# Eight blocks of attention and an FP8 layer: POOL's order, two additions and the last layer's engines changed

## The chip, the cores and the metric

One core of one Trainium2 chip runs the whole program. Its engines work in parallel, each on its own list in order: PE (matrix multiplication, with weight loads listed as PEld), DVE (vector), ACT (scalar activations), POOL (GpSimd) and SP, which only issues transfers. Semaphores order them. The metric is the device time of one execution in microseconds (us).

## The reference, cut to what matters

```python
x = x + attention0(layernorm(x), ctx)
x = x + experts(layernorm(x))                      # top 2 of 8, gated MLP
# second attention, 16 heads of 16, 77 keys, on q = layernorm(x)
Qp = q @ Wq + bq;  Q = Qp / norm(Qp);  K = l2norm(ctx @ Wk + bk);  V = ctx @ Wv + bv
y = softmax(Q K^T * SCALE) V @ Wo + bo + Qp
x = x + (y - mean(y)) / sqrt(var(y) + eps) * gamma + beta
# last layer: FP8 matrix product, result rounded to bf16
xf = layernorm(x);  x8, sx = quant_fp8(xf);  w8, sw = quant_fp8(W)
x = x + ((x8 @ w8.T) * (sx * sw) + bias).astype(bfloat16)
```

x is 4 x 1024 tokens of 256 channels in f32, and stays on the chip as `g["x"]` (`x_res` in the trace).

## The kernel before, in words

The tokens are cut into `NBLK` = 8 blocks of 512 (`TJ` = 4 tiles of 128 tokens), two blocks to a batch (`BPB` = 2). The change touches two functions, `attention1` and `quantized_ffn`. Each writes, engine by engine, a fixed order of work for block n.

In `attention1` the blocks overlap. While PE works through the ten score and value steps (c = 0 to 9) of block n, it also projects the queries of block n+1 (`pe_queries`, L1805, c = 0 and 1), spreads the softmax sums of block n-1 (`pe_spread`, L1824, c = 2 to 4), transposes the queries of n+1 (`pe_transpose_q`, c = 4 and 5, L1783), makes the outputs of n-1 (`pe_outputs`, L1816, c = 5 and 6) and transposes the layer norm of n+2 (`pe_transpose_x`, c = 7 and 8, L1783). All transposes share one bank `tr`, so the second transpose waits until DVE's split (`dve_split`, L1949) has read the first (semaphore `tr_lo`).

DVE's order for block n (`dve_block`) is: shift of the last norm of n-3 (L2026), reciprocal of the sums (L1976), `dve_queries` (L1972) and `dve_combine` (L1957: adds the gathered experts' rows) in turns, the divides (L1984, L1988), statistics, `dve_shift` (L1966), the two query splits, maximum of the last norm (L2030), the residual of block n-1 (L1995), its statistics and gamma (L2009), one split of n+2, `dve_update` (L2017: x += y * rstd) and the other split. `dve_shift` waits for POOL's `gp_ln`.

POOL's order (`gp_block`) is: in the first block of a batch `gp_keys(.., 1)` (L2114, block-diagonal keys), `gp_beta` of n-1 (L2105), `gp_root` (L2095), in the second block of a batch `gp_keys(.., 0)`, four indirect gathers (L2084), `gp_ln` (L55, L57), four gathers, `gp_last_rstd`, `gp_residual` (L2101: qres = qp + bo) and `gp_y` (the 1/std of y). PE's order is not touched.

In `quantized_ffn`, for block n: ACT scales xf into v (`scaled`, L2290); DVE masks out the exponent (`power`, L2331); ACT makes of it the rounding constant (`round_at`, L2294); DVE adds and subtracts it (`rounded`, L2336 and L2339); PE transposes in f32 (L2380); ACT copies to bf16 (`copy_qT`, L2301); PE multiplies (L2391); DVE scales and adds the bias (`finish`, L2348); POOL adds to x (L2365); SP stores the block. v has three buffers, e, qT and z two each. ACT's order in one round is:

```python
round_at(n + 1)
scaled(n + 2)
copy_qT(n)
```

Of the kernel before, what the change touches and what calls it, by code (L numbers as in the profile page):

```python
# [1718 lines left out]
def attention1(nc, g, xd):  # L1719

    with ExitStack() as ctx:
# [198 lines left out]
        def act_block(act, n):  # L1920
            for c in range(NC3):
# [6 lines left out]
                if n > 2 and c in (0, 2):  # L1928
                    act_last_norm(act, n - 3, c // 2)
                if n < LAST and c in (1, 2):  # L1930
                    act_squares(act, n + 1, c - 1)
                if n < LAST and c == 3:
                    act_unit_queries(act, n + 1)
                if c == 4:
                    act_raw(act, n, 0)
# [32 lines left out]
        def dve_queries(dve, n, a):  # L1968
            dve.wait_ge(s["proj_mm"], proj_count(n, 0, a))
            if a == 0 and n >= 2:  # L1970
                dve.wait_ge(s["qres_ready"], n - 1)
            dve.tensor_tensor(pair(qp[n % 2], a), banked(proj), two_tiles(g["bq1"]), ALU.add).then_inc(s["proj_out"], 1)  # L1972

# [59 lines left out]
        def dve_block(dve, n):  # L2033
            nxt, nxt2, prv, prv2, prv3 = n < LAST, n + 1 < LAST, n > 0, n > 1, n > 2
            if prv3:
                dve_last_shift(dve, n - 3)
            if prv:
                dve_inverse_sums(dve, n - 1)
            if nxt:
                dve_queries(dve, n + 1, 0)  # L2040
            if nxt2:
                dve_combine(dve, n + 2, 0)
# [4 lines left out]
            if prv:  # L2047
                dve_divide(dve, n - 1, 0)
# [6 lines left out]
            if nxt2:  # L2055
                dve_shift(dve, n + 2)
            if prv:
                dve_divide(dve, n - 1, 2)
            if nxt:
                dve_split(dve, n + 1, 1, 0, qT[(n + 1) % 2])  # L2060
                dve_split(dve, n + 1, 1, 1, qT[(n + 1) % 2])
            if prv3:
                dve_last_max(dve, n - 3)
            if prv:
# [14 lines left out]
        def gp_gather(gp, n, ks=range(TOP_K)):  # L2079
            if n >= 2 and ks[0] == 0:  # L2080
                gp.wait_ge(s["both_added"], n - 1)
            for k in ks:
                for j in range(TJ):
                    gp.indirect_dma_start(out=routed[n % 2][:, k, j, :], out_offset=None, in_=xd,  # L2084
                                          in_offset=bass.IndirectOffsetOnAxis(ap=g["slots"][:, n, k, j:j + 1], axis=0)).then_inc(gathered[n % 2], 16)
# [12 lines left out]

        def gp_residual(gp, n):
            gp.wait_ge(s["proj_out"], max(proj_count(n, 0, 1), proj_count(n - 2, 1, 1) if n >= 2 else 0))  # L2100
            gp.tensor_tensor(qres[n % 2][:, :, :], qp[n % 2][:, :, :], four_tiles(g["bo1"]), ALU.add).then_inc(s["qres_ready"], 1)  # L2101

        def gp_beta(gp, n):
            gp.wait_ge(s["xn_ready"], n + 1)
            gp.tensor_tensor(g["x"][:, n, :, :], g["x"][:, n, :, :], four_tiles(g["beta"]), ALU.add).then_inc(s["beta_added"], 1)  # L2105
# [17 lines left out]
        def gp_block(gp, n):  # L2123
            nxt, nxt2, prv, prv2 = n < LAST, n + 1 < LAST, n > 0, n > 1
            if n % BPB == 0 and n:
                gp.wait_ge(s["score_mm"], NC3 * n)
                gp_keys(gp, n // BPB, 1)
            if prv:
                gp_beta(gp, n - 1)
# [5 lines left out]
            if n + 3 <= LAST:  # L2135
                gp_gather(gp, n + 3, range(0, 1))
            if nxt2:
                gp_ln(gp, n + 2)
            if n + 3 <= LAST:
                gp_gather(gp, n + 3, range(1, TOP_K))  # L2140
            if prv2:
                gp_last_rstd(gp, n - 2)
            if prv:
                gp_residual(gp, n)
                gp_y(gp, n - 1)

        with nc.Block() as block:  # L2147
            @block.gpsimd
            def _(gp):
# [8 lines left out]
                gp_residual(gp, 0)  # L2158
                for n in range(NBLK):
                    gp_block(gp, n)  # L2160
                gp_beta(gp, LAST)
# [28 lines left out]
            def _(dve):  # L2190
# [6 lines left out]
                for a in range(2):  # L2197
                    dve_queries(dve, 0, a)
                for k in range(TOP_K):
# [16 lines left out]
                for a in range(2):  # L2216
                    dve_residual(dve, LAST, a)
                    dve_y_stats(dve, LAST, a)
                    dve_gamma(dve, LAST, a)
                dve_update(dve, LAST)  # L2220
# [24 lines left out]

def quantized_ffn(nc, g, w, out):

    with ExitStack() as ctx:
        sb = lambda name, shape, dt: ctx.enter_context(nc.sbuf_tensor(name, shape, dt))
        pb = lambda name: ctx.enter_context(nc.psum_tensor(name, [P, 512], F32))  # L2250
        bias = sb("ffn_bias", [P, D], F32)
# [5 lines left out]
        qT = [sb(f"ffn_qT{s}", [P, DC, TB], BF16) for s in range(2)]  # L2257
        z = [sb(f"ffn_z{s}", [P, TJ, D], BF16) for s in range(2)]
        tr = [pb(f"ffn_tr{s}") for s in range(2)]
# [3 lines left out]
                 "tr_mm", "qT_out", "mm", "z_out", "x_done", "stored")  # L2263
        s = {n: ctx.enter_context(nc.semaphore(n + "4")) for n in names}

# [6 lines left out]
        with nc.Block() as block:  # L2272
            @block.sync
            def _(sp):
                sp.dma_start(bias[:, :], w["L1_ffn_bias"].partition_broadcast(P)).then_inc(s["bias_in"], 16)
# [6 lines left out]

            @block.scalar
            def _(act):
                def scaled(n):
                    if n >= 3:
                        act.wait_ge(s["tr_mm"], DC * (n - 2))
# [6 lines left out]
                def copy_qT(n):  # L2296
                    if n >= 2:
                        act.wait_ge(s["mm"], 2 * n - 2)
                    for dc in range(DC):
                        act.wait_ge(s["tr_mm"], DC * n + dc + 1)  # L2300
                        act.activation(qT[n % 2][:, dc, :], tr[dc][:, :], ACT.Copy).then_inc(s["qT_out"], 1)  # L2301

                act.wait_ge(s["limit_done"], 8)
                scaled(0)
                round_at(0)
                scaled(1)
                for n in range(NBLK):
# [4 lines left out]
                    copy_qT(n)  # L2312

            @block.vector
            def _(dve):
# [9 lines left out]
                dve.wait_ge(s["bias_in"], 16)  # L2325
# [8 lines left out]
                def rounded(n):  # L2334
                    dve.wait_ge(s["m_ready"], n + 1)
                    dve.scalar_tensor_tensor(values(v[n % 3]), values(e[n % 2]), ROUND_AT * FP8_MIN_NORMAL, values(v[n % 3]),  # L2336
                                             ALU.add, ALU.add).then_inc(s["t_done"], 1)
                    dve.wait_ge(s["t_done"], n + 1)
                    dve.scalar_tensor_tensor(values(v[n % 3]), values(e[n % 2]), ROUND_AT * FP8_MIN_NORMAL, values(v[n % 3]),  # L2339
                                             ALU.add, ALU.subtract).then_inc(s["q_ready"], 1)  # L2340

                def finish(n):
                    if n >= 2:
                        dve.wait_ge(s["x_done"], n - 1)
                    for a in range(2):
                        dve.wait_ge(s["mm"], 2 * n + a + 1)
                        for b in range(2):
                            last = dve.scalar_tensor_tensor(z[n % 2][:, 2 * a + b, :], acc[2 * (n % 2) + a][:, b * D:(b + 1) * D],  # L2348
                                                            dequant[:, 0:1], bias[:, :], ALU.mult, ALU.add)
                        last.then_inc(s["z_out"], 1)  # L2350

                power(0)
                for n in range(NBLK + 1):
                    if n + 1 < NBLK:
                        power(n + 1)
                    if n < NBLK:
                        rounded(n)
                    if n >= 1:
                        finish(n - 1)

            @block.gpsimd
            def _(gp):
                for n in range(NBLK):
                    gp.wait_ge(s["z_out"], 2 * n + 2)
                    gp.tensor_tensor(g["x"][:, n, :, :], g["x"][:, n, :, :], z[n % 2][:, :, :], ALU.add).then_inc(s["x_done"], 1)  # L2365

            @block.tensor
            def _(pe):
# [3 lines left out]
                ffn_spread_scales(pe, g, small, scale_row, s["small_mm"])  # L2372

                def transposes(n):
                    pe.wait_ge(s["q_ready"], n + 1)
                    for dc in range(DC):
                        if n >= 1:
                            pe.wait_ge(s["qT_out"], DC * (n - 1) + dc + 1)
# [74 lines left out]
```

## Time and profile before

| what | us |
|---|---|
| median of 3 runs | 1111.58 (1111.31 to 1115.03) |
| the profiled execution | 1118.64 |
| span of its instructions | 1116.8 |
| second attention, first to last block's PE work | about 757 to 1016 of the span |
| its tail, until the last layer begins | to 1053.8 |
| last layer, until its last addition ends | 1053.8 to 1113.8 |
| store of the last block | to 1116.8 |

Times in the rows count from the start of the span. Mean duration overlaps for neighbouring instructions; the step from start to start is what a series costs.

### The profile page before, as it was taken

How to read it: one execution, taken by the hardware profiler on the slowest of the kernel's cores; microseconds unless marked ns; L12 is line 12 of the kernel's file. 1: busy time of each engine (PE TensorE's matmuls, PEld its weight loads, DVE VectorE, ACT ScalarE, POOL GpSimd, SP SyncE). 2: the span in 40 equal slices, each digit the busy share in tenths (PEclk: the TensorE clock that was granted, in tenths of full speed). 3: DMA queues.
4: the chain of work that ended last, by engine and by line, in shares of the span. 5: the costliest groups of instructions: out<-in, count | busy, mean ns of one | idle time of the engine just before them, and what ended most of it. 6: DMA issues, size and time to landing. Idle time of an engine off the chain costs nothing. (4 is left out here: it accounts for less than half of the span.)

```text
span 1116.8 us, 17792 instructions
## 1 busy us (share of the span) xinstructions
PE 937.9 (84%) x5479; PEld 776.5 (70%) x5479; DVE 795.3 (71%) x1838; ACT 536.7 (48%) x1471; POOL 393.6 (35%) x418
## 2 busy tenths in 40 slices
PE   5999999999997999989999975337979889996254
PEld 5899999999996888878999965224445545543143
DVE  6788788788875678766777765333488688777497
ACT  4676566665664554424444431025545465642252
POOL 3243234243343365450000012464455665222024
PEclk9899999999999899999999996558899899997555
DMA  9999910000000343223344332120001110000012
GB/s 304 286 304 301 301 49 0 0 0 0 0 1 29 95 132 114 92 75 105 119 121 127 119 112 44 54 58 24 28 25 38 38 38 1 0 1 1 5 56 95
DMA packets 52758, 91.97 MB, mean 82 GB/s; under 512 B 5350, under 2 KB 27726, under 8 KB 52686
## 3 DMA queue, kind: packets, MB, share of 16 engines
q1 hardware_dynamic: 46542, 74.29, 22.2%
q0 software_dynamic: 6144, 16.79, 4.7%
q8 instruction: 38, 0.62, 0.2%
q14 instruction: 34, 0.28, 0.1%
HBM read 34.69 MB, written 56.36 MB: 82 GB/s over the span
## 5 line engine op out<-in xcount | busy, mean ns | idle before, releaser
L462 POOL TENSOR_TENSOR prob<-prob,row_inv 128x462 f32<-128x462 f32 (+1 forms) x96 | 83.6, 874 | 184.9 <-DVE row_inv L623 184.9
L794 PE MATMUL acc<-u,probT 128*128 128x256 f32 (+1 forms) x960 | 133.5, 289 | 0.9 <-DVE u L635 0.9
L522 ACT ACTIVATE prob<-score,neg_max 128x77 f32<-128x77 f32 x512 | 120.6, 348 | 13.2 <-DVE neg_max L617 12.9
L748 PE MATMUL score<-m,xnT 128*128 128x462 f32 (+1 forms) x576 | 124.8, 355 | 0.0
L794 PEld LDWEIGHTS acc<-u,probT 128*128 128x128 f32 (+1 forms) x960 | 119.4, 189 | 1.9 <-DVE u L635 1.4
L748 PEld LDWEIGHTS score<-m,xnT 128*128 128x128 f32 x576 | 97.7, 191 | 6.3
L1057 PE MATMUL py<-w1T,hidT 128*128 x426 | 92.6, 353 | 0.0
L1324 POOL DMA_INDIRECT dispatched<-xn,slots x64 | 68.7, 1073 | 61.0 <-DVEq L1189 43.9
L512 ACT ACTIVATE probT<-tr 128x512 fp32r<-128x512 f32 (+1 forms) x96 | 51.5, 541 | 68.7 <-PE tr L734 68.5
L1835 PE MATMUL score<-qT,kbd 128*128 128x512 f32 (+1 forms) x240 | 80.2, 444 | 2.1 <-ACT prob L1903 2.1
L2084 POOL DMA_INDIRECT routed<-dispatched,slots x64 | 62.4, 975 | 40.8 <-SPq L2147 22.9
L1057 PEld LDWEIGHTS py<-w1T,hidT 128*128 128x128 f32 x426 | 71.8, 191 | 0.2 <-issue 0.2
L617 DVE TENSOR_REDUCE neg_max<-score 128x6 f32<-128x462 f32 (+1 forms) x96 | 55.8, 581 | 17.4 <-PE score L748 16.9
L1846 PE MATMUL acc<-prob,va 128*102 128x512 f32 x128 | 66.9, 606 | 0.0
L612 DVE TENSOR_TENSOR probT<-tr,probT 128x512 fp32r<-128x512 f32 (+1 forms) x96 | 56.5, 592 | 14.0 <-ACT probT L512 13.6
L1835 PEld LDWEIGHTS score<-qT,kbd 128*128 128x128 f32 (+1 forms) x240 | 41.7, 193 | 30.0 <-ACT prob L1903 15.5
L1611 POOL MEMSET head_rows<- 128x616 f32 x1 | 0.6, 611 | 166.9 <-POOLq L1327 166.9
L621 DVE TENSOR_REDUCE row_sum<-prob 128x6 f32<-128x462 f32 (+1 forms) x96 | 55.3, 576 | 3.0 <-ACT prob L522 2.1
L1903 ACT ACTIVATE prob<-score 128x512 f32<-128x512 f32 (+1 forms) x80 | 45.8, 584 | 16.8 <-PE score L1835 16.8
L734 PE MATMUL tr<-ident,prob 128*128 128x128 f32 x320 | 50.0, 272 | 1.0 <-DVE probT L612 1.0
L1135 ACT ACTIVATE gated<-py 128x192 f32<-128x192 f32 x71 | 23.5, 331 | 41.1 <-PE py L1057 41.1
L734 PEld LDWEIGHTS tr<-ident,prob 128*128 128x128 f32 x320 | 38.9, 138 | 6.0 <-issue 1.2
(323 smaller groups left out, 2273.9 us busy)
## 6 DMA issues: line engine op xcount, KB each, us to landing
dispatched<-zeros SPq DMA_DIRECT2D x1, 33664.0 KB, 118.6
xn<-dispatched SPq DMA_DIRECT2D x71, 128.0 KB, 2.1
dispatched<-hid SPq DMA_DIRECT2D x71, 128.0 KB, 1.7
out<-x_res SPq DMA_DIRECT2D x8, 512.0 KB, 2.6
x_res<-in_x SPq DMA_DIRECT2D x1, 3072.0 KB, 15.2
w_stage<-in_L_ffn_W SPq DMA_DIRECT2D x8, 384.0 KB
w_stage<-in_L_ffn_Ws SPq DMA_DIRECT2D x3, 384.0 KB
x_res<-in_x SPq DMA_DIRECT2D x2, 512.0 KB, 10.1
```

Source lines behind the costliest of these rows:

```text
L462: gp.tensor_tensor(pr, pr, row_inv[t % 2][:, heads(k)].unsqueeze(2).to_broadcast([P, BANK_HEADS[k], KEYS]), ALU.mult).then_inc(prob_ready, 1)
L522: last = act.activation(prob[t % 2][:, h * KEYS:(h + 1) * KEYS], score_of(t, k)[:, n * KEYS:(n + 1) * KEYS], ACT.Exp, bias=neg_max[t % 2][ ...
L612: dve.tensor_tensor(probT[t % 2][1][:, c0:c0 + n, :], tr_of("p", t, gr)[:, 0:n * P].rearrange("p (c q) -> p c q", q=P), f32(probT[t % 2][0 ...
L617: dve.tensor_reduce(neg_max[t % 2][:, heads(k)], scores_of(t, k), AX_X, ALU.max, negate=True).then_inc(max_ready, 1)
L734: last = pe.transpose(tr_of("p", t, gr)[0:w, (c - c0) * P:(c - c0 + 1) * P], prob[t % 2][:, c * P:c * P + w], g["ident"][:, :])
L748: last = pe.matmul(score_of(t, k)[:, 0:BANK_HEADS[k] * KEYS], xnT[blk][i][:, dc, j * P:(j + 1) * P], m[w][:, dc, cols(k)], start=(n == 0 a ...
L794: last = pe.matmul(acc[t % 2][:, 0:D], probT[t % 2][i][0:rows, c, :], u[k][0:rows, c, :], start=(c == 0 and q == 0), stop=(c == KCH - 1 an ...
L1057: last = pe.matmul(py[i % 2][:, 0:UP], xtT[i % 2][m][:, dc, :], w1[k][:, dc, ds(expert, 1), :].rearrange("p a h -> p (a h)"), start=(q == ...
L1324: gp.indirect_dma_start(out=xd, out_offset=bass.IndirectOffsetOnAxis(ap=g["slots"][:, n, k, j:j + 1], axis=0), in_=xn[n % XN_BUFS][:, j, : ...
L1835: last = pe.matmul(score[c % 2][0:rows, :], keys, qT[n % 2][k][:, f, :], start=(q == 0), stop=(q == 2))
L1846: last = pe.matmul(acc[f][0:A_COLS, :], g["va"][0:rows, b, f, cc, :], p, start=(cc == 0), stop=(cc == A_LAST))
L2084: gp.indirect_dma_start(out=routed[n % 2][:, k, j, :], out_offset=None, in_=xd, in_offset=bass.IndirectOffsetOnAxis(ap=g["slots"][:, n, k, ...
```

## The change

1. `attention1`, additions: `gp_beta` and `gp_residual` go. DVE makes both in one instruction each: `dve_query_residual(n)` before the first divide, `dve_beta(n-1)` after the second gamma. For block 0 the residual stands ahead of DVE's combine of block 1.
2. `attention1`, POOL's order: the second keys wait also for `x_done` (the update before). In the second block of a batch no gather stands ahead of `gp_ln`; in others two, not four. `gp_y` comes ahead of the last gathers of a second block and ahead of `gp_last_rstd`.
3. `attention1`, DVE and ACT order: `dve_last_shift` after the first queries, `dve_shift` between the two query splits (it was ahead of both); on ACT the last norm goes from c = 0, 2 to c = 1, 3, behind squares and unit queries.
4. `quantized_ffn`: rounding writes bf16 (`q`), transposes are bf16 into a bf16 bank of 1024 columns, all eight ahead of one semaphore; ACT copies them in one instruction and also applies the scale and writes z. The bias enters through PE as a third matmul per tile, from three bf16 pieces that POOL makes of it once. DVE adds z to x. PE's order is `transposes(n)` and then `products(n-1)`.

```diff
 def dve_block(dve, n):
-    if prv3: dve_last_shift(dve, n - 3)
     if prv: dve_inverse_sums(dve, n - 1)
     if nxt: dve_queries(dve, n + 1, 0)
+    if prv3: dve_last_shift(dve, n - 3)
...
     if prv:
+        dve_query_residual(dve, n)
         dve_divide(dve, n - 1, 0)
...
-    if nxt2: dve_shift(dve, n + 2)
     if prv: dve_divide(dve, n - 1, 2)
     if nxt: dve_split(dve, n + 1, 1, 0, qT[(n + 1) % 2])
+    if nxt2: dve_shift(dve, n + 2)
     if nxt: dve_split(dve, n + 1, 1, 1, qT[(n + 1) % 2])
...
         dve_gamma(dve, n - 1, 1)
+        dve_beta(dve, n - 1)
 def gp_block(gp, n):
     if n % BPB == 0 and n:
+        gp.wait_ge(s["x_done"], n - 1)
         gp.wait_ge(s["score_mm"], NC3 * n)
         gp_keys(gp, n // BPB, 1)
-    if prv: gp_beta(gp, n - 1)
     if nxt: gp_root(gp, n + 1)
-    if nxt and n % BPB == BPB - 1:
+    if turn:                               # nxt and n % BPB == BPB - 1
         gp.wait_ge(s["score_mm"], NC3 * n + C3)
         gp_keys(gp, n // BPB + 1, 0)
-    if n + 3 <= LAST: gp_gather(gp, n + 3, range(0, 1))
+    elif nxt3: gp_gather(gp, n + 3, 0, 2)
     if nxt2: gp_ln(gp, n + 2)
-    if n + 3 <= LAST: gp_gather(gp, n + 3, range(1, TOP_K))
+    if nxt3: gp_gather(gp, n + 3, 0 if turn else 2, 6 if turn else TOP_K * TJ)
+    if prv: gp_y(gp, n - 1)
+    if nxt3 and turn: gp_gather(gp, n + 3, 6)
     if prv2: gp_last_rstd(gp, n - 2)
-    if prv:
-        gp_residual(gp, n)
-        gp_y(gp, n - 1)
 # quantized_ffn, POOL (was: x += z for every block)
+    gp.memset(bias_rows[:, :], 0.0); gp.memset(minus_one[:, :], -1.0)
+    gp.wait_ge(s["limit_done"], 7)
+    gp.tensor_scalar(part, bias, scales[0:1, 0:1], g["ffn_w_scales"][0:1, 0:1], ALU.mult, ALU.mult)
+    for n, at in enumerate(BIAS_AT):       # (0, 32, 64); each step waits for the one before
+        gp.tensor_copy(piece[n], part)
+        gp.tensor_copy(bias_rows[at:at + 1, :], piece[n])
+        if n + 1 < len(BIAS_AT): gp.tensor_tensor(part, part, piece[n], ALU.subtract)
 # ACT, one round
     round_at(n + 1); scaled(n + 2); copy_qT(n)
+    if n: finish(n - 1)    # 2 x activation(z, acc, ACT.Copy, scale=dequant), 128x512
 # DVE, one round
-    power(n + 1); rounded(n); finish(n - 1)
+    rounded(n); power(n + 2); add(n - 2)   # add: x = x + z, 128x1024
 # PE, products(n), for each of four tiles
     for dc in range(DC): matmul(bank, qT[n % 2][:, j, dc, :], g["ffn_wqT"][:, dc, :], ...)
+    if n == 0 and j == 0: pe.wait_ge(s["part_step"], PART_STEPS)   # 9
+    matmul(bank, minus_one[:, :], bias_rows[:, :], start=False, stop=True)
 # PE, one round
-    products(n - 1); transposes(n)
+    transposes(n); products(n - 1)
```

## Rows read from the trace of the kernel before

**Rows 1.** Windows, six blocks of the second attention, a tail stretch, the last layer.

```profile
core 0: us, PE busy (x) PEld busy (x) DVE busy (x) ACT busy (x) POOL busy (x), PEclk, DMA share, GB/s
764.98:793.99 29.01, 25.15 (x95) 14.70 (x95) 9.84 (x24) 15.26 (x36) 12.73 (x13) 0.88 0.12 36
793.99:829.33 35.34, 29.98 (x118) 16.97 (x117) 26.03 (x47) 17.03 (x38) 22.11 (x20) 1.00 0.10 31
829.33:861.27 31.94, 29.91 (x116) 16.81 (x117) 27.07 (x56) 15.70 (x36) 17.55 (x18) 1.00 0.12 33
861.27:899.85 38.58, 32.64 (x117) 18.97 (x117) 28.89 (x57) 18.34 (x41) 23.32 (x22) 0.91 0.10 28
899.85:931.89 32.04, 30.16 (x117) 16.72 (x117) 27.65 (x57) 18.21 (x41) 17.56 (x18) 1.00 0.11 34
931.89:964.41 32.52, 30.02 (x116) 16.81 (x117) 28.77 (x57) 18.21 (x41) 15.37 (x14) 1.00 0.00 1
1030.00:1040.00 10.00, 7.58 (x17) 5.00 (x16) 5.24 (x11) 2.07 (x4) 0.00 (x0) 0.50 0.00 0
1053.80:1113.80 60.00, 31.34 (x131) 21.34 (x131) 49.85 (x66) 26.47 (x32) 19.79 (x8) 0.50 0.16 64
```

**Rows 2.** Waits of PE, 764 to 1012: total us, times, longest.

```profile
PE tr L1783 <- DVE qT L1949: 11.3, 5, 3.5
PE proj L1805 <- DVE xnT L1949: 5.8, 5, 1.6
PE proj L1805 <- DVE qp L1972: 2.8, 5, 0.6
```

**Rows 3.** Timeline of DVE: start us, us, then the idle time before and its releaser.

```profile
811.19 0.16 DVE L1966 SCALAR_TENSOR_TENSOR shift<-mean_var,rstd 128x4 f32<-128x4 f32 x1 [5.28 <-POOL rstd L57]
...
856.75 3.77 DVE L2017 SCALAR_TENSOR_TENSOR x_res<-y,rstd_y,x_res 128x256 f32<-128x256 f32 x4
...
893.05 6.05 DVE L2017 SCALAR_TENSOR_TENSOR x_res<-y,rstd_y,x_res 128x256 f32<-128x256 f32 x4
...
1043.30 1.67 DVE L2017 SCALAR_TENSOR_TENSOR x_res<-y,rstd_y,x_res 128x256 f32<-128x256 f32 x4 [0.50 <-POOL rstd_y L57]
```

**Rows 4.** Timeline of POOL beside those updates.

```profile
856.69 2.37 POOL L2105 TENSOR_TENSOR x_res<-x_res,beta 128x1024 f32<-128x1024 f32 x1
...
892.98 2.93 POOL L2114 TENSOR_TENSOR kbd<-k1T,head_rows 128x616 fp32r<-128x616 f32 x2
```

**Rows 5.** Groups by form: busy us, mean ns of one.

```profile
L1663 DVE TENSOR_TENSOR k<-k,kinv 77x1024 f32<-77x1024 f32 x1 | 1.2, 1222 | 0.0
...
L1400 POOL CAST first_row<-first_i 1x71 f32<-1x71 int32 x1 | 0.2, 233 | 0.0
```

**Rows 6.** Timeline of ACT and PE, start and tail of the second attention.

```profile
754.06 2.08 ACT L1894 ACTIVATE xn<-x_res,shift,rstd 128x256 f32<-128x256 f32 x4 [3.66 <-DVE shift L1966]
...
1022.38 2.01 PE L1824 MATMUL wide<-oinv,spread_sum 6*96 6x512 f32 x2 [6.32 <-DVE oinv L1976]
```

**Rows 7.** Timeline of the last layer, all engines.

```profile
1061.42 1.22 DVE L2336 SCALAR_TENSOR_TENSOR ffn_v<-ffn_e,ffn_v 128x1024 f32<-128x1024 f32 x1
1061.53 1.15 ACT L2294 ACTIVATE ffn_e<-ffn_e,floor 128x1024 f32<-128x1024 f32 x1 [0.76 <-DVE ffn_e L2331]
1063.95 1.97 PE L2380 MATMUL ffn_tr<-ident,ffn_v 128*128 128x128 f32 x8 [7.76 <-DVE ffn_v L2339]
1065.95 0.60 ACT L2301 ACTIVATE ffn_qT<-ffn_tr 128x512 bf16<-128x512 f32 x1 [0.26 <-PE ffn_tr L2380]
1066.61 1.89 PE L2391 MATMUL ffn_acc<-ffn_wqT,ffn_qT 128*128 128x256 bf16 x8 [0.69 <-ACT ffn_qT L2301]
...
1069.33 0.68 DVE L2331 TENSOR_SCALAR ffn_e<-ffn_v 128x1024 int32<-128x1024 int32 x1
1069.49 2.50 POOL L2365 TENSOR_TENSOR x_res<-x_res,ffn_z 128x1024 f32<-128x1024 f32 x1 [21.27 <-DVE ffn_z L2348]
1069.93 3.15 DVE L2336 SCALAR_TENSOR_TENSOR ffn_v<-ffn_e,ffn_v 128x1024 f32<-128x1024 f32 x1
...
1111.67 2.12 POOL L2365 TENSOR_TENSOR x_res<-x_res,ffn_z 128x1024 f32<-128x1024 f32 x1 [1.82 <-DVE ffn_z L2348]
```

**Rows 8.** Timeline of PE: where the clock rose, and where it did not.

```profile
757.39 1.12 PE L1783 MATMUL tr<-ident,qn 128*128 128x128 f32 x4 [5.82 <-DVE qT L1949]
758.16 2.81 PE L1835 MATMUL score<-qT,kbd 128*128 128x512 f32 x6
...
1031.62 3.75 PE L1816 MATMUL proj<-wo1f,oT 128*128 128x256 f32 x8 [1.57 <-DVE oT L1988]
1036.23 3.78 PE L1816 MATMUL proj<-wo1f,oT 128*128 128x256 f32 x8 [0.85 <-DVE y L1995]
```

More of the change, by code:

```diff
@@ L1933, in act_block @@
                     act_unit_queries(act, n + 1)
+                if n > 2 and c in (1, 3):
+                    act_last_norm(act, n - 3, c // 2)
                 if c == 4:
@@ L2076, in dve_block, with gp_gather @@
                 dve_split(dve, n + 2, 0, 1, xnT)
-        def gp_gather(gp, n, ks=range(TOP_K)):
-            if n >= 2 and ks[0] == 0:
+        def gp_gather(gp, n, first=0, last=TOP_K * TJ):
+            if n >= 2 and first == 0:
                 gp.wait_ge(s["both_added"], n - 1)
[L2082 to L2085, printed above, removed]
+            for k, j in (divmod(i, TJ) for i in range(first, last)):
+                gp.indirect_dma_start(out=routed[n % 2][:, k, j, :], out_offset=None, in_=xd,
+                                      in_offset=bass.IndirectOffsetOnAxis(ap=g["slots"][:, n, k, j:j + 1], axis=0)).then_inc(gathered[n % 2], 16)
         def gp_ln(gp, n):
@@ L2250, in quantized_ffn @@
         pb = lambda name: ctx.enter_context(nc.psum_tensor(name, [P, 512], F32))
-        bias = sb("ffn_bias", [P, D], F32)
+        bias, part = sb("ffn_bias", [1, D], F32), sb("ffn_bias_part", [1, D], F32)
+        piece = [sb(f"ffn_bias_piece{i}", [1, D], BF16) for i in range(len(BIAS_AT))]
+        bias_rows, minus_one = sb("ffn_bias_rows", [BIAS_END, D], BF16), sb("ffn_minus_one", [BIAS_END, P], BF16)
+        ident = sb("ffn_ident", [P, P], BF16)
         amax, limit, scale_row = ffn_scale_buffers(sb, "x")
@@ L2311, in _ @@
                         scaled(n + 2)
-                    copy_qT(n)
+                    if n < NBLK:
+                        copy_qT(n)
+                    if n:
+                        finish(n - 1)
             @block.vector
@@ L2340, in rounded, with add @@
+                    dve.scalar_tensor_tensor(values(q[n % 2]), values(e[n % 2]), ROUND_AT * FP8_MIN_NORMAL, values(v[n % 3]),
                                              ALU.add, ALU.subtract).then_inc(s["q_ready"], 1)
[L2342 to L2350, printed above, removed]
+                def add(n):
+                    dve.wait_ge(s["z_out"], 2 * n + 2)
+                    dve.tensor_tensor(x_values(g["x"], n), x_values(g["x"], n), values(z[n % 2]), ALU.add).then_inc(s["x_done"], 1)
@@ L2352, in _ @@
                 power(0)
-                for n in range(NBLK + 1):
-                    if n + 1 < NBLK:
-                        power(n + 1)
+                power(1)
+                for n in range(NBLK + 2):
                     if n < NBLK:
                         rounded(n)
[L2358 to L2365, printed above, removed]
+                    if n + 2 < NBLK:
+                        power(n + 2)
+                    if n >= 2:
+                        add(n - 2)
```

128 lines of the change are left out of this document (80 added, 48 removed).

## The prediction, made before the changed kernel was run

> **What bounds the kernel now.** I cut the span into stages with the windows view and read which wait ends last in the two stages that the change touches. In the second attention [rows 1] PE is busy 25.15 to 32.64 us of blocks that last 29 to 38.6 us, so PE sets the pace and what can be won is its idle time. Over the six blocks: 3.9, 5.4, 2.0, 5.9, 1.9 and 2.5 us. The clock column adds to this: it is 0.88 in the first and 0.91 in the fourth block. The fourth does the same work as its neighbours but is busy 32.64 us against about 30.0, so 2.6 us are work at 1.2 in place of 2.4 GHz, right behind one of the long gaps; the first lost about as much (0.12 of 29 us at half speed, some 3). PE's waits name three causes [rows 2]: the query transpose waits for DVE's split (11.3 us in 5 waits), the projection waits for the split of the layer norm (5.8) and for the reading of its bank (2.8).
>
> The timeline of DVE says why DVE is late. `dve_shift` sits ahead of the query splits and waits up to 5.28 us for POOL's rstd [rows 3], behind keys and four gathers. And `dve_update` takes 1.67 us at the end, where POOL is idle, but 3.77 beside POOL's 2.37 us addition of beta, and 6.05 beside keys and beta together [rows 3, 4]: POOL's large two-input instructions hold DVE up nearly for their whole length (2.1 of 2.37 us; 4.4 of about 5.3, the two of them one behind the other). The Trainium skill (GPSIMD Engine Reference, 1. Specifications) says that POOL shares its SBUF interfaces with DVE instructions that read two SBUF inputs; by that rule the trace agrees, 3.77 against 1.67 us.
>
> In the last layer (60 us) DVE is busy 49.85, PE 31.34 at half clock, ACT 26.47 [rows 1]. DVE sets its pace, and it too is held up: the first rounding step takes 1.22 us alone and 3.15 beside POOL's 2.50 us addition [rows 7].
>
> **The change, part by part: second attention.**
> *Shift moved.* The first query split no longer stands behind POOL. Of the first, second and fourth block it frees 2.6, 3.4 and 3.4 us of PE (most of the 11.3 [rows 2]; the rest, twice 0.8, is a divide that the shift had delayed). With the gaps the two stretches at the low clock go: 2.2 and 2.6 us (of the 3 in the first block I count 2.2).
> *Additions moved to DVE.* The trace has no such DVE instruction; the nearest is a two-input f32 multiply of 77x1024, 1.22 us [rows 5], 1.15 from start to start. Per block DVE gets 2.3 us and loses 2.1 (update without beta), and 4.4 in the three blocks where keys stood there too, as the keys now wait for the update. So the split behind the update comes 2.1 - 1.15 = 0.95 us earlier in a common block, 4.4 - 1.15 = 3.2 in those three. The waits of the projection there were 0.4 to 0.6 and 1.6 us long [rows 2], and the 0.6 us wait for the bank follows from the same lateness: all 8.6 us can go. The residual lies where DVE waited for PE's spread anyway. If POOL's keys meet it, it grows; lower bound 1.15, upper 1.15 + 2.1.
> *New bound.* I took DVE's list of the fifth block (32.0 us from reciprocal to reciprocal, about 27.6 busy [rows 1]) and put the change in: 32.0 + 2.3 - 2.1 - 1.2 (a gamma that had run beside the residual) - 0.8 (shift wait) = 30.2 us, against PE's 30.2. A tie, so I leave each block 0.4 to 0.8 us above PE's sum. Gains by block: 4.8, 5.1, 1.4, 7.6, 1.5, 1.9, and 0.7 for the seventh, sum 23.0. Two engines that are both full make waits that I don't see; I take 15% off: 19.5.
> *Start.* Ahead of block 0, the residual stands in front of combine(1), statistics, shift and ACT's norm, for which ACT waited 3.66 us before it could copy the queries [rows 6]: all path, +1.15.
> *Tail.* PE waits 6.32 us for the reciprocal behind the update of block 6 [rows 6]. Beta costs 1.15 there, hides the 0.5 that the update waited for POOL, and the update falls by 2.1: -1.45. In block 7 beta is new on the path, less the same 0.50 [rows 3]: +0.65. Net -0.8.
> *Gathers.* 2 of 8 now come behind `gp_y` in a second block; they start about 2 us ahead of the next block and are needed 4 us into it, so 6 us cover two issues of 1.26 and their landing. Costed at nothing; uncovered, they would add up to 2 us in two blocks. The keys are needed by step c = 5, some 15 us off: nothing. ACT's moved norm: nothing, its consumer stands last.
> Second attention: -19.5 + 1.15 - 0.8 = -19.2.
>
> **Last layer.** Prices, start to start [rows 7]: scaled S and round_at R 1.05 (seen 1.15 later), DVE power 0.6 (0.68), rounding pair 2.5 (2 x 1.22), add 1.15 (as above), copy C of 1024 columns 1.05 (S's size; two of 0.60 were 1.2), finish F twice 0.6. Products: 8 matmuls took 1.89 us, so 12 take 2.75. Transposes: unseen in bf16. Upper bound the f32 row, 1.97; lower bound half a 256-column bf16 matmul each (1.89/16 x 8 = 0.95). I take 1.1, near the lower, as the bf16 matmul row fits the type.
> I laid these on the four lists by hand. DVE's own sum is 4.3 us a block and ACT's 4.15, but a loop through all engines is longer: S(n) ends, power 0.7, add 1.1, rounded(n-1) 2.55, transposes 1.1, products(n-2) 2.7, its F 0.5, R 1.05, S(n+2) 1.15 = 10.85 us for two blocks, 5.4 each, where now it is 60/8 = 7.5 with start and end, 6.5 in between. The stamps, in the old span's time: first rounding done 1062.25 (it was 1063.9), S(6) done 1082.85, rounded(6) 1091.55, rounded(7) 1095.25, transposes(7) 1096.5, products 1101.9, last F 1102.5, last addition 1103.7. Before it was 1111.67 + 2.12 = 1113.8 [rows 7]: -10.1.
> *Bias pieces.* Nine steps of POOL, 256 elements each: between 0.23 us (a 1x71 cast [rows 5]) and 0.6 (a quarter of 2.37 [rows 4]) plus 0.1. They end 3.0 to 6.3 us behind 1056.4, ahead of the first products at 1066.6, so PE doesn't wait. But they run beside the first rounding (from 1059.75) and may hold it up by 0 to 2.5 us. I take 1.5, as the rounding has two SBUF inputs like the update: -8.6 in all.
>
> **Sum.** -19.2 - 8.6 = -27.8. On the profiled execution 1118.64 - 27.8 = 1090.8; that one lies 7.1 us above the median of the runs, and I take the same difference off the median: 1111.58 - 27.8 = 1083.8.
>
> **The rivals.**
> *R1, PE's clock rises in the last layer.* New rounds give PE two runs of 3.8 us with a 0.6 us gap, then 2.7 idle. For it: ahead of the first block PE worked from 757.39 to 760.97 without a gap, and the first block then starts at the high clock. Against it: two runs of 3.75 and 3.78 us with a gap of 0.85 stayed at 0.50 [rows 8, 1], the nearer picture. With the clock up, transposes save 0.5 and products 1.35 per two blocks of the loop, 4 x 1.85 = 7.4, and some 1.5 in the tail: about 1075. The Trainium skill (TensorE: Matmul & The Clock Gate, What's actually happening) says that activity releases the throttle; by that rule both rows can be read, since the second is broken up.
> *R2, only part of the waits goes.* DVE with 29 us in 30.2 becomes the bound and gives half of the 23 back, or the last layer's transposes cost 1.97 (+0.9 x 4 + 0.9 = 4.5): 1089 to 1100. For it the tie of 30.2 and 30.2; against it the three big gaps, which don't depend on DVE's load.
> *R3, the other side: the additions on DVE are stretched themselves.* They read two SBUF inputs, and POOL still makes keys. If they were held up in every block to 3.3 us each (1.2 + 2.1), DVE would gain 6.6 and lose 2.1: +4.5 in seven blocks, +31, against -10 (shift), -5 (clock), -8.6: 1119. It decides from 3.4 us net per block ((10 + 5 + 8.6)/7). Against it: POOL's large instructions after the change are only the keys, 2.7 us in six places, so most blocks have nothing that could do it. By the skill's rule above, the sum would be 3 x 2.1 = 6 us worse at most.
> *R4, nothing that can be measured*: a new wait per block of 3 to 4 us in POOL's list (for `x_done`, or `gp_y` ahead of gathers) that eats the gain.
>
> **How the numbers follow.** The forecast (1077 to 1091 its own range) 0.56; R1 0.15; R2 0.19; R3 and other losses 0.05; R4 0.05. The range leaves out 1 in 10 above and the far end of R1 below: 1073 to 1098. A difference under 0.5% (5.6 us) can't be told from none. Faster than 1106: 0.90; within 0.5%: 0.05; slower: 0.05.
>
> **What would show it.** In the second attention: PE's waits for the query split near 0 (were 11.3), clock 1.00 in all blocks, blocks of 30 to 31 us, the update at 1.67 throughout. In the last layer: rounds of 5.4 us, both rounding steps at 1.22 but for the first block, PEclk 0.50. Wrong: the update still over 3 us; additions over 2 us; DVE's share over 0.95 with PE waiting on it; rounds of 6 us or more, or a last layer at clock 1.00.

## The result, and the profile after

The changed kernel takes 1072.2 us (median of 4 runs, 1068.67 to 1077.18) against 1113.3 for the kernel before beside it: ratio 0.9634, 95% interval 0.9589 to 0.968. Timed again in another set it was 1080.3 against 1116.2, ratio 0.9658 (0.9633 to 0.9682). So it gains 36 to 41 us where 27.8 were forecast; the first median lies 0.8 us under the range.

The profiled execution took 1071.32 us. The second attention, from its first gather to the maximum that opens the last layer (`x_amax`), took 344.1 us before and 319.1 after; the last layer, from there to its last addition, 60.0 and 46.8. That makes -38.1 us. The code ahead of the first gather is the same in all kernels; that gather started at 709.7 us before, at 700.4 here, and at 703.6 to 711.3 in the twelve other profiles. So the 9.3 us between the two profiles there can't be put down to the change.

Windows of the changed kernel, its first six blocks by the first projection of each, and the last layer (compare [rows 1]):

```profile
756.94:781.32 24.38, 22.23 (x95) 13.39 (x95) 9.83 (x24) 15.25 (x36) 10.34 (x12) 1.00 0.15 44
781.32:811.09 29.77, 29.55 (x119) 16.87 (x117) 23.71 (x49) 15.99 (x37) 16.81 (x18) 1.00 0.12 36
811.09:840.99 29.90, 29.70 (x119) 16.90 (x117) 25.53 (x57) 16.17 (x38) 14.71 (x17) 1.00 0.13 36
840.99:871.01 30.02, 29.81 (x119) 16.81 (x117) 26.65 (x59) 18.14 (x42) 16.81 (x19) 1.00 0.12 36
871.01:901.00 29.99, 29.78 (x118) 16.79 (x117) 26.60 (x59) 18.08 (x42) 15.97 (x18) 1.00 0.12 36
901.00:931.02 30.02, 29.77 (x119) 16.83 (x117) 26.64 (x59) 18.10 (x41) 10.31 (x12) 1.00 0.00 1
1019.56:1066.41 46.85, 21.53 (x163) 15.82 (x163) 36.47 (x42) 34.87 (x41) 8.41 (x11) 0.75 0.18 70
```

Read the second and third number of each line together. From the second block on PE is busy for all but 0.2 us of a block, at full clock; in the first it is still idle for 2.15 us, 1.6 of them in one gap. Against [rows 1] the blocks gained 4.6, 5.6, 2.0, 8.6, 2.1 and 2.5 us, 25.4 in all.

PE's waits in the second attention (compare [rows 2], which begins later, at the first block). The 7.1 us of the first line, 2.8 of the second, the 1.4 and the 0.8 stand ahead of that block; behind it 0.3 us are left of the first line and 0.5 of the second:

```profile
PE tr L1783 <- DVE qT L1949: 7.4, 2, 7.1
PE tr L1783 <- DVE xnT L1949: 3.3, 5, 1.4
PE proj L1805 <- DVE xnT L1949: 1.4, 1, 1.4
PE proj L1805 <- DVE qp L1972: 0.8, 1, 0.8
```

DVE's timeline, the end of one block: beta, the two splits and the update between them (compare [rows 3]), and POOL's line that answers to [rows 4], the keys that now wait for the update:

```profile
925.81 1.21 DVE L1980 TENSOR_TENSOR x_res<-x_res,beta 128x1024 f32<-128x1024 f32 x1
926.94 0.68 DVE L1949 TENSOR_TENSOR xnT<-tr,xnT 128x512 fp32r<-128x512 f32 x1
927.54 1.66 DVE L2025 SCALAR_TENSOR_TENSOR x_res<-y,rstd_y,x_res 128x256 f32<-128x256 f32 x4
929.25 0.69 DVE L1949 TENSOR_TENSOR xnT<-tr,xnT 128x512 fp32r<-128x512 f32 x1
```

```profile
929.28 2.73 POOL L2116 TENSOR_TENSOR kbd<-k1T,head_rows 128x616 fp32r<-128x616 f32 x2 [1.12 <-DVE x_res L2025]
```

The update takes 1.66 or 1.67 us in every block, the new additions 1.21 to 1.23.

The start and the tail, ACT and PE (compare [rows 6, 8]):

```profile
746.08 2.07 ACT L1894 ACTIVATE xn<-x_res,shift,rstd 128x256 f32<-128x256 f32 x4 [4.97 <-DVE shift L1966]
```

```profile
987.36 2.02 PE L1824 MATMUL wide<-oinv,spread_sum 6*96 6x512 f32 x2 [4.98 <-DVE oinv L1984]
...
996.60 3.75 PE L1816 MATMUL proj<-wo1f,oT 128*128 128x256 f32 x8 [1.57 <-DVE oT L1996]
1001.21 3.78 PE L1816 MATMUL proj<-wo1f,oT 128*128 128x256 f32 x8 [0.85 <-DVE y L2003]
```

From first gather to first projection of block 1 it is 56.5 us, against 55.3; from 931.0 to `x_amax` 88.5, against 89.4.

The last layer, two rounds of ACT and the transposes beside them (compare [rows 7]):

```profile
1037.20 1.14 ACT L2316 ACTIVATE ffn_v<-xf,scales 128x1024 f32<-128x1024 f32 x1
1038.24 1.01 ACT L2326 ACTIVATE ffn_qT<-ffn_tr 128x1024 bf16<-128x1024 bf16 x1
...
1042.64 0.98 PE L2408 MATMUL ffn_tr<-ffn_ident,ffn_q 128*128 128x128 bf16 x8 [4.96 <-DVE ffn_q L2377]
...
1045.00 0.69 ACT L2333 ACTIVATE ffn_z<-ffn_acc,dequant 128x512 bf16<-128x512 f32 x1 [0.32 <-PE ffn_acc L2424]
...
1046.97 0.62 PE L2408 MATMUL ffn_tr<-ffn_ident,ffn_q 128*128 128x128 bf16 x8 [0.79 <-DVE ffn_q L2377]
...
1047.84 1.14 ACT L2316 ACTIVATE ffn_v<-xf,scales 128x1024 f32<-128x1024 f32 x1
```

From the first `ffn_v` to the last shown two blocks take 10.64 us. They are a slow round and a quick one: DVE's second rounding step starts 6.33 us behind the one before it, then 4.33. In the slow round PE does its transposes at the low clock (0.98 us at 1042.64, behind a wait of 4.96), in the quick one at the high clock (0.62 at 1046.97). The three stretches of the last layer, up to the first rounds, the body, and behind the last rounding step:

```profile
1022.56:1034.56 12.00, 3.63 (x25) 2.87 (x26) 10.08 (x10) 9.41 (x10) 7.78 (x9) 0.50 0.00 0
1034.56:1060.56 26.00, 13.89 (x105) 9.93 (x103) 20.71 (x20) 21.44 (x26) 0.00 (x0) 0.84 0.24 97
1060.56:1066.56 6.00, 3.27 (x32) 2.65 (x32) 4.06 (x4) 3.34 (x5) 0.00 (x0) 1.00 0.35 141
```

The clock did not stay at 0.50: it moves between its two levels (1.2 and 2.4 GHz) in the body and is at the high one in the tail.

### The profile page after: what moved, and what is told of

Same layout as the page of the kernel before. It is cut to its first block and busy times, and to the rows that moved or that the text cites. A ratio compares the mean times of both kernels' runs of the same rounds, so it can differ in the third digit from the quotient of the medians.

```text
span 1069.6 us, 17855 instructions
## 1 busy us (share of the span) xinstructions
PE 916.8 (86%) x5511; PEld 764.3 (71%) x5511; DVE 775.9 (73%) x1830; ACT 544.2 (51%) x1480; POOL 350.9 (33%) x405
## 5 line engine op out<-in xcount | busy, mean ns | idle before, releaser
L522 ACT ACTIVATE prob<-score,neg_max 128x77 f32<-128x77 f32 x512 | 121.0, 351 | 11.6 <-DVE neg_max L617 11.3
L1324 POOL DMA_INDIRECT dispatched<-xn,slots x64 | 70.2, 1097 | 55.9 <-DVEq L1189 38.8
L612 DVE TENSOR_TENSOR probT<-tr,probT 128x512 fp32r<-128x512 f32 (+1 forms) x96 | 56.5, 592 | 14.0 <-ACT probT L512 13.6
L621 DVE TENSOR_REDUCE row_sum<-prob 128x6 f32<-128x462 f32 (+1 forms) x96 | 55.3, 576 | 3.1 <-ACT prob L522 2.2
```

The costliest lines, as they stand in the source:

```text
L522: last = act.activation(prob[t % 2][:, h * KEYS:(h + 1) * KEYS], score_of(t, k)[:, n * KEYS:(n + 1) * KEYS], ACT.Exp, bias=neg_max[t % 2][ ...
L612: dve.tensor_tensor(probT[t % 2][1][:, c0:c0 + n, :], tr_of("p", t, gr)[:, 0:n * P].rearrange("p (c q) -> p c q", q=P), f32(probT[t % 2][0 ...
L1324: gp.indirect_dma_start(out=xd, out_offset=bass.IndirectOffsetOnAxis(ap=g["slots"][:, n, k, j:j + 1], axis=0), in_=xn[n % XN_BUFS][:, j, : ...
```

## The experiments

Stage times below are as above, from one profile each: second attention, last layer (344.1 and 60.0 in the kernel before; 319.1 and 46.8 in the changed kernel, 318.8 and 46.9 when it was profiled again).

**The two halves alone.**

```diff
 # first run: attention1 as changed, quantized_ffn as before
 # second run: attention1 as before, quantized_ffn as changed
```

> The second attention as changed, the last layer as before. Theory A (the gains of the two stages are separate and add): the second attention, from its first gather to the start of the last layer, takes 319 us as in the changed kernel (344 before), the last layer 60 us as before; in all 25 us less than before, a ratio near 0.978. Theory B (the forecast's tie: the two full engines leave only 19 us to win, and the rest of the measured gain came from elsewhere): stage of 325 us, ratio 0.983. Theory C (the 9 us that the untouched stages differ by in the two profiles belong to the change): they differ here again by about 9 us.

> The last layer as changed, the second attention as before. Theory A (the stages add): last layer 47 us, second attention 344 us, in all 13 us less than before, ratio 0.988. Forecast's size: 51.4 us, ratio 0.992. Theory C (untouched stages belong to the change): they are 9 us shorter here too.

Measured: 1090.74 us (ratio 0.9803, 0.9775 to 0.983), stages 318.9 and 60.0; and 1098.76 (0.9872, 0.9842 to 0.9901), stages 340.9 and 47.1. Beside them the kernel before had 1114.12. The halves don't touch each other: -23.4 and -15.4 make -38.8. Each is more than its part of the forecast, 19.2 and 8.6. The 340.9 us are the attention of the kernel before, unchanged, and 3.2 less than in its other profile: PE's clock was 0.88 in the first block there and 1.00 here, and the second output projection of the tail took 3.78 us there and 1.99 here. Against this profile the attention gained 22.0 us and not 25.0. The second run's last layer also shows what the clock is worth in it:

```profile
1060.58:1086.58 26.00, 17.49 (x103) 12.32 (x102) 20.56 (x20) 20.97 (x25) 0.00 (x0) 0.57 0.23 94
1086.58:1092.58 6.00, 3.99 (x36) 2.83 (x34) 4.29 (x4) 4.24 (x7) 0.00 (x0) 0.93 0.34 139
```

The body ran at 0.57 in place of 0.84 and the layer took 47.1 us in place of 46.8. What differs is the quick rounds: their transposes took 1.03 us here and 0.62 there, where PE had time to spare. The slow rounds had theirs at the low clock in both.

**The shift's old place.**

```diff
+    if nxt2: dve_shift(dve, n + 2)        # ahead of the last divide and both splits again
     if prv: dve_divide(dve, n - 1, 2)
-    if nxt2: dve_shift(dve, n + 2)        # it stood between the splits
 # POOL: gp_ln behind four gathers in every block again
```

> The changed kernel with two parts of the order undone: the shift stands ahead of the last divide and both query splits again, and four gathers stand ahead of POOL's layer norm. Theory A (the split waited for POOL's rstd): PE's wait for the query split comes back, about 11 us in five waits (the changed kernel has 0.3 us there after block 0's start), with one or two stretches at the low clock, and the second attention takes 330 to 333 us in place of 319. Rival B (the moved additions alone had made DVE late, and with them settled the shift has slack): under 3 us more.

Measured: 1089.57 us, second attention 333.5, 14.4 more. One block of it, and PE's waits:

```profile
852.59:887.70 35.11, 31.03 (x119) 17.99 (x117) 26.86 (x59) 18.23 (x42) 16.90 (x19) 0.95 0.10 31
```

```profile
PE tr L1783 <- DVE qT L1949: 20.1, 6, 7.1
```

The waits for the query split go from 7.4 to 20.1 us, and with each of the two longest (3.9 us) PE does the same work in 31.0 to 31.2 us in place of 29.8 or less, at clock 0.95. These two parts of the order, the shift's place and POOL's gathers, were undone together, so their shares are not known; together they are worth over half of the 25 us.

**Both additions on POOL, in the new order.**

```diff
-    dve_query_residual(dve, n); dve_beta(dve, n - 1)
 # gp_block, behind the second keys, and ahead of gp_y
+    if prv: dve_beta(gp, n - 1)
+    if prv: dve_query_residual(gp, n)
```

> The changed kernel with beta and the residual made by POOL again, the rest of the order as changed. Theory A (POOL's large two-input instructions hold DVE's updates up): the update takes 3.8 us beside beta and 1.7 nowhere but at the end, PE waits for the split of the layer norm and for its bank come back, 5 to 9 us in all, second attention 324 to 328 us. Rival B (with the keys moved away from the update, DVE has the slack to bear 2.1 us): the updates are long but PE waits under 2 us, second attention 319 to 321 us. Rival C (the additions cost DVE more than they give back): under 319 us.

Measured: 1077.75 us, second attention 315.7, 3.5 less than with DVE's additions. My theory, that the update would be held up again, was wrong. DVE's update, two of its gammas, POOL's beta and residual, and the block that grew most:

```profile
838.40 2.37 DVE L2017 SCALAR_TENSOR_TENSOR y<-y,mean_var_y,gamma 128x256 f32<-128x256 f32 x2
...
843.96 1.67 DVE L2025 SCALAR_TENSOR_TENSOR x_res<-y,rstd_y,x_res 128x256 f32<-128x256 f32 x4
...
898.58 3.51 DVE L2017 SCALAR_TENSOR_TENSOR y<-y,mean_var_y,gamma 128x256 f32<-128x256 f32 x2
```

```profile
845.29 2.58 POOL L1980 TENSOR_TENSOR x_res<-x_res,beta 128x1024 f32<-128x1024 f32 x1
...
899.04 2.36 POOL L1976 TENSOR_TENSOR qres<-qp,bo 128x1024 f32<-128x1024 f32 x1
```

```profile
877.56:908.60 31.04, 29.48 (x119) 16.87 (x117) 28.22 (x57) 17.99 (x40) 22.76 (x21) 1.00 0.12 35
```

Before, `gp_y` was POOL's last work in a block; it released the update and POOL went straight to beta. In the new order `gp_last_rstd` stands between, and in the blocks with second keys those wait for the update and beta stands behind them. Beta starts 1.33 us behind the update, near its end, and doesn't hold it up. The collisions moved elsewhere: four of the gammas beside POOL's residual took 1.65 to 3.51 us, where 0.9 is usual, and two shifts of the last norm 1.94 and 2.32 in place of 0.15. With DVE's additions all of these took 0.88 to 0.92 and 0.10 to 0.16. All in all the six blocks grew by 1.0 us; the 3.5 us less lie ahead of them and in the tail, and the last comparison below says why.

**The keys don't wait for the update.**

```diff
     if n % BPB == 0 and n:
-        gp.wait_ge(s["x_done"], n - 1)
```

> The changed kernel without the wait for the update ahead of POOL's second keys, so that the keys come back beside the update in three blocks. Theory A (large two-input POOL work beside the update is what stretched it): the update of those three blocks takes 3.5 to 4.5 us in place of 1.67. If the split behind it sets PE's start, the second attention grows by 3 to 6 us (319 to 322 to 325); if DVE has 2 us of slack there, it stays at 319 to 320 though the update is long.

Measured: 1082.46 us, second attention 324.9. Two of the three updates concerned are held up; the first, and POOL's keys beside it:

```profile
814.88 4.76 DVE L2025 SCALAR_TENSOR_TENSOR x_res<-y,rstd_y,x_res 128x256 f32<-128x256 f32 x4
...
937.14 3.94 DVE L2025 SCALAR_TENSOR_TENSOR x_res<-y,rstd_y,x_res 128x256 f32<-128x256 f32 x4
```

```profile
816.61 2.73 POOL L2116 TENSOR_TENSOR kbd<-k1T,head_rows 128x616 fp32r<-128x616 f32 x2
```

Those blocks last 31.7 and 31.2 us in place of 29.8 and 30.0. The stretch ahead of block 1 takes 29.4 in place of 27.5, at clock 0.50, but it took 29.3 and 29.4 in two profiles with the attention as changed as well; so the wait for `x_done` is worth 3.8 us of the 5.8 (from block 1 to block 7, 177.9 us in place of 174.1). The middle update kept its 1.66 us: two gathers and `gp_last_rstd` stood ahead of the keys there, which began 3.06 us behind it. In the other two only the gathers or only `gp_last_rstd` stood between, and the keys began 1.73 and 0.59 us behind the update. So a delay alone is no sure remedy: beta, in the experiment above, began 1.33 us behind the update and left it alone, and the keys at 1.73 did not.

The update ends 0.3 us behind the end of the keys. The Trainium skill (SBUF — State Buffer, Who interferes with whom) says that a DVE instruction with two SBUF inputs and a POOL instruction that reads SBUF exclude each other, and that the order of issue decides which of the two waits. On the first point these rows agree. The order can't be read from them: of the update's four instructions the last was held up (3.57 us), and the profile has it start at 816.06, 0.55 us ahead of the keys.

**Four more additions on DVE.**

```diff
     dve_beta(dve, n - 1)
+    for i in range(4): dve.tensor_tensor(spare, two_tiles(gamma), two_tiles(bo1), ALU.add)   # 128x512
```

> The changed kernel with four more two-input additions of 128x512 on DVE, each waiting for the one before, behind beta in every block from the second on: about 2.8 us of DVE work a block that nobody needs. The forecast's step (DVE and PE are tied at 30.2 us, so every us on DVE is a us of the block): blocks of 32.5 to 33 us in place of 30.0, second attention 335 to 340 us. Theory A (DVE's waits for PE shrink as it gets later, DVE is busy 26.6 of 30 us and PE alone sets the block): blocks of 30.0 to 31 us, second attention 320 to 326 us.

Measured: 1108.36 us, second attention 345.8, 26.6 more, above both of my ranges. One block (from 822.0), and PE's waits over four blocks:

```profile
822.00:856.00 34.00, 31.07 (x116) 17.72 (x116) 28.06 (x61) 16.27 (x36) 16.80 (x18) 0.95 0.12 35
```

```profile
PE tr L1785 <- DVE xnT L1951: 11.7, 4, 2.9
```

The four add 2.8 us of DVE's time and the block grows by 4.1: the split behind them is late by 2.9, where PE had waited for it 0.3 us in four blocks together, and the other 1.2 are PE's lower clock behind the gap. DVE is busy 26.6 of 30 us in the changed kernel and has all the same nothing to spare at this place. The tie that the prediction worked out (30.2 against 30.2) was real at this place; it cost nothing by itself.

**In the last layer, ScalarE's order and PE's clock.**

```diff
 # first run: six idle products a round, into a bank of their own
     products(n - 1)
+    for _ in range(6): matmul(warm, ffn_wqT[:, 0, 0:128], ffn_wqT (512 columns))
 # second run: finish one block later
-    copy_qT(n); finish(n - 1)
+    finish(n - 2); copy_qT(n)
```

> The changed kernel with six bf16 matmuls of 512 columns into a spare bank behind each block's products in the last layer, to fill PE's idle time; they change no result. If PE's clock, which goes up and down there (1.2 GHz in the transposes and products behind each long gap), costs time on the loop through all engines: the clock stays high from the third block on and the last layer takes 42 to 44 us in place of 46.9. If the high clock is not kept, or the filling delays the transposes: 48 to 52 us.

> The changed kernel with ACT finishing block n-2 ahead of the copy of block n, where it finished n-1 behind it; so ACT no longer waits for products that PE has just begun. If the loop through all engines (10.6 us for two blocks) sets the pace of the last layer, and not the clock or DVE's own sum: rounds of 4.4 to 4.6 us (DVE's sum 4.3), last layer 40 to 43 us in place of 46.9. If DVE or ACT alone was the bound already: 46 to 47.5 us.

Measured: 1075.86 us with a last layer of 44.3 us, and 1081.07 with 43.7, each a little above the range I had for its theory. The body of each in two windows of 10 us, from 15 us behind `x_amax` on (first run, then second):

```profile
1041.62:1051.62 10.00, 7.23 (x57) 4.52 (x55) 8.12 (x8) 9.18 (x13) 0.00 (x0) 1.00 0.16 66
1051.62:1061.62 10.00, 6.67 (x53) 4.23 (x52) 9.12 (x10) 9.28 (x11) 0.00 (x0) 1.00 0.34 137
```

```profile
1047.43:1057.43 10.00, 6.90 (x45) 4.79 (x43) 8.78 (x9) 9.36 (x12) 0.00 (x0) 0.67 0.22 88
1057.43:1067.43 10.00, 7.42 (x45) 5.22 (x45) 9.35 (x10) 9.23 (x12) 0.00 (x0) 0.55 0.31 123
```

With the clock up all through the body, the layer gains 2.5 us. All of it lies in two slow rounds, 7.03 and 6.33 us before, 5.96 and 4.89 now; the quick ones stay at 4.33, DVE's own sum. What the idle products cost by standing ahead of the next transposes was not measured apart. With the finish behind the next block's work the rounds are 4.33 and 4.71 us at a clock of 0.55 to 0.67, with DVE busy 0.9 of the time: ScalarE's waits for PE's products, 2.4 us in the body of the changed kernel, are gone, and with them, as the last comparison shows, nearly all that the clock could give.

**POOL adds z to x in the last layer.**

```diff
-    add(n - 2)                            # DVE
+    for n in range(NBLK): ...             # waits for both halves of z(n), then
+                          gp.tensor_tensor(x[n], x[n], z[n % 2], ALU.add)   # POOL, behind the bias pieces
```

> The changed kernel, but in the last layer POOL adds z to x again, as before the change, in place of DVE. Theory: the addition on POOL (2.1 to 2.5 us) holds up DVE's rounding steps (3.15 in place of 1.22 us), so that DVE gains 1.2 us a block and loses about 2: last layer 50 to 54 us in place of 46.9, with rounding steps above 2.5 us in most blocks. Rival: the loop through ScalarE and PE sets the round (DVE is busy 7.1 to 7.7 of 10 us), so the stretching is hidden and the last layer stays at 46 to 49 us.

Measured: 1085.16 us, last layer 50.05, at the low end of my range, and not for its reason. Only one rounding step met an addition:

```profile
1065.75 3.15 DVE L2380 SCALAR_TENSOR_TENSOR ffn_q<-ffn_e,ffn_v 128x1024 bf16<-128x1024 f32 x1
```

```profile
1065.70 2.12 POOL L2312 TENSOR_TENSOR x_res<-x_res,ffn_z 128x1024 f32<-128x1024 f32 x1 [1.67 <-ACT ffn_z L2336]
...
1076.13 4.20 POOL L2312 TENSOR_TENSOR x_res<-x_res,ffn_z 128x1024 f32<-128x1024 f32 x2 [0.66 <-ACT ffn_z L2336]
```

The last rounding step ended 41.0 us into the layer, 0.5 earlier than with DVE's additions; the loss is the end, 9.0 us behind it in place of 5.3. Of these 3.7 us the two slower additions are 1.8 (4.20 against 2.38); the rest goes with PE's clock, 0.82 there and 1.00 in the changed kernel. In the runs with the shift's old place and with four more additions the last layer was unchanged, and its end took 6.1 us at clock 0.86: 0.8 us for the clock alone.

**A version from the parts that won, and the changed kernel beside it.** The first is the changed kernel as it is, the second has both additions on POOL and the later finish, the third the idle products besides.

> The changed kernel once more, untouched, as the measure for the two versions beside it. If the 41 us that it won over the kernel before (1113.3 to 1072.2) are its stages' 38.1 us (344.1 to 319.2 and 60.0 to 46.9) and 3 us of chance in the parts ahead of the second attention, this run gives 1074 to 1077 against 1114. If the change itself made those early parts shorter, it gives 1070 to 1072, and the second attention begins at 700 us again; by chance it begins anywhere from 700 to 711.

> The changed kernel with two edits at once: POOL makes both additions again (as in the run that put the second attention at 315.6 us, 3.6 less than the change), and ScalarE finishes block n-2 ahead of the copy of block n (which put the last layer at 43.8 us, 3.1 less). If both hold, the time is 6 to 7 us under the changed kernel timed beside it, a ratio near 0.994 to it, attention stage 315 to 317 and last layer 43.8. If the 3.6 us were the chance of one look (its clock rose once early, ahead of the first block, worth about 1.3), attention stays at 318 to 319 and the gain is 3 to 4 us.

> The same two edits and six idle matrix products (512 columns each, into a bank of their own) behind the products of every round of the last layer. Alone they took 2.5 us off the last layer (46.9 to 44.4), the later finish 3.1. If both work on the same loop (the products' time ahead of ScalarE's finish), they don't add: the last layer stays at 43 to 44 us, near DVE's own sum of 4.3 us a block, or gets longer because the idle products stand ahead of the next transposes. If they are separate: 41.3 us.

| kernel | us, median | ratio to before (1116.2) | second attention | last layer |
|---|---|---|---|---|
| as changed | 1080.32 (5 runs) | 0.9658 (0.9633 to 0.9682) | 318.8 | 46.9 |
| additions on POOL, later finish | 1076.51 (5 runs) | 0.9638 (0.9616 to 0.9659) | 317.3 | 43.7 |
| the same, idle products | 1074.85 (6 runs) | 0.9612 (0.9589 to 0.9636) | 319.8 | 43.2 |

The untouched changed kernel came out above the 1074 to 1077 us that I had expected; its stages are those of the first profile, and its second attention began at 710.1 us. The last layer keeps its 3 us; the idle products add 0.5 more, not 2.5, as DVE now goes round in 4.33 us, its own sum. The 3.5 us of the attention don't hold: with the additions on POOL the stage came out at 315.7, 317.3 and 319.8. The difference between these is where the clock rises. In the last of them the two output projections at the tail took 3.75 and 3.78 us, as in the changed kernel; in the other two the second took 1.99. And in the first of them the stretch ahead of block 1 took 24.9 us at clock 0.73, in the other two 26.5 and 26.6. The third version has no such luck; against the changed kernel profiled beside it, it saves 0.7 us up to block 1 (PE waits 5.82 for the query split, not 7.13) and loses 1.1 in the blocks and 0.5 in the tail. The intervals of the first and the third version overlap by 0.0003; the second's overlaps with both.

## Why the prediction was right or wrong

The direction, the places and most of the mechanisms were right; the gain was forecast 10 us too small, against 38 in the traces. By its steps:

- *Shift moved*: right. 11.3 us of waits became 0.3, the stretches at the low clock went, and putting it back, with POOL's gathers, cost 14.4 us, against 9.4 + 4.8 forecast.
- *Additions moved to DVE*: price right (1.21, and 1.13 from start to start), the update right (1.66 everywhere), cause wrong. I put the 2.1 us a block that the update lost down to the beta on POOL, and so to its move. With beta on POOL and POOL's new order the update is 1.67 too. The gain belongs to the order and to the wait of the keys; what the move itself saves in the six blocks is 1.0 us, all of it in the block whose gamma took 3.51.
- *New bound*: this is the step that failed. "Two engines that are both full make waits that I don't see; I take 15% off", and "I leave each block 0.4 to 0.8 us above PE's sum". No row showed those waits, and they didn't come: all blocks but the first stand 0.2 us above PE's sum, and the six gained 25.4 us where 19.5 were counted: 5.9 us.
- *Start* +1.26 (forecast 1.15), *tail* -0.9 (-0.8), gathers and ACT's norm nothing: right. Together -25.0 where -19.2 stood.
- *Last layer*, the schedule by hand: 10.64 us for two blocks where 10.85 were written down, and the last rounding step ended 41.5 us in, where the stamps say 41.5 without the bias. *Bias pieces*: POOL's nine steps took 8.5 us, over my bound of 6.3, and still ended ahead of the first products. They ran beside two roundings, but held them up by 0.1 to 0.2 us a step and not by 1.5 in all; the first rounding ended 8.6 us in, against 8.5 by the undisturbed stamps. That term was 1.3 us too high.
- *R1, the clock rises in the last layer*, had 0.15 and came true where it was priced least. In the tail the transposes and two sets of products ran at the high clock: the last addition ended 5.3 us behind the last rounding step in place of 8.45, so 3.1. R1 had "some 1.5" there, though its own prices for one set of transposes and two of products (0.5 and twice 1.35) make 3.2. In the body the clock went up and down and gave next to nothing (0.84 or 0.57: 46.8 or 47.1), as it was up in the rounds that DVE sets; kept up artificially it gave 2.5 us, not the 7.4 of the rival. There the row of two broken-up runs at 0.50 [rows 8], which I held to be the nearer picture, did not carry over.
- R2 (1089 to 1100) fell: none of the big gaps nor DVE's load gave back anything. R3: the additions on DVE were not held up; R4: the wait for `x_done` cost POOL 1.12 us that nobody waited for.

5.9 + 1.3 + 3.1 = 10.3 us, against 38.1 - 27.8 = 10.3. That it closes so well is in part the choice of profile. Against the other profile of the old attention (340.9 us) the six blocks gained 23.7 and the stage 22.0, and the first term would be 4.2; the stages of that profile and of the last layer's two make 35, near the 35.9 of the second set. The clock's turns in the old attention are worth 3 us of this account, and two profiles can't say which is usual. The other 3 us of the first measured difference (41.1) lie ahead of the touched code; the second set has 35.9, with that code at 710.1 us. Which transfer or wait makes that part start the gathers at 700 or at 711 us was not tried.

One thing stays open: the additions' owner. With the clock's luck taken out the two versions are within about a microsecond, which these profiles can't decide.

## What to carry to other kernels

If a trace shows an instruction stretched beside another engine's, look first at what releases both. Here one semaphore started the update and freed POOL for its next large instruction. For beta small work between the two was enough; for the keys it was not in two blocks of three, and a wait for the update kept them clear in all. Where the schedule by hand said that two engines tie, the trace showed no wait; take off for unseen waits only what a row shows, and test the edge with a little added load instead. And price a clock by the place where it rises: in rounds that DVE set it was worth nothing, in rounds that waited for PE up to 1.4 us each, and in the tail, where all waits for PE, about 3 us against the forecast.

## What the runs showed of the hardware

- A gap can cost twice. In two experiments seven blocks with a gap of 2.9 to 3.9 us, in which PE waited for DVE, also had work at the lower clock worth another 1.2 to 1.6 us (31.07 in place of 29.8 us busy, clock 0.95). It isn't certain: in the kernel before, the second block of [rows 1] had a gap of 3.5 us and stayed at clock 1.00, and the fourth with the same gap lost 2.6 us.
- The clock doesn't repeat where PE's work is broken up: with the same instructions the stretch ahead of block 1 took 27.2 to 29.4 us in the profiles of kernels with this attention, and in the attention of the kernel before the same output projection took 3.78 us in one profile and 1.99 in the other. Single profiles of a stage differ by 2 to 3 us for this alone.
- The size of a held-up DVE instruction says little: beside POOL's keys a shift of 128x4 values took 1.34 us in the changed kernel (0.15 elsewhere):

```profile
744.71 1.34 DVE L1966 SCALAR_TENSOR_TENSOR shift<-mean_var,rstd 128x4 f32<-128x4 f32 x1 [1.43 <-POOL rstd L57]
```

- Between a POOL chain of 1x256 values and DVE's 128x1024 roundings both pay, POOL more: its copy took 0.87 us, and 1.28 beside a rounding, while the rounding took 1.38 in place of 1.22:

```profile
1023.41 0.87 POOL L2307 COPY ffn_bias_rows<-ffn_bias_piece 1x256 bf16<-1x256 bf16 x1
...
1025.79 1.28 POOL L2307 COPY ffn_bias_rows<-ffn_bias_piece 1x256 bf16<-1x256 bf16 x1
```

```profile
1025.42 1.38 DVE L2373 SCALAR_TENSOR_TENSOR ffn_v<-ffn_e,ffn_v 128x1024 f32<-128x1024 f32 x1
```
